# An FFN kernel with LoRA experts: two transposes per pair of token tiles moved from TensorE to VectorE and SBUF transfers

## The chip, the cores and the metric

The kernel runs on one core of a Trainium2 chip. The metric is the device time of one execution in microseconds (us). The kernel before takes 154.13 us, the median of 3 runs (153.89 to 154.21).

## The reference, cut to what matters

There are 2048 tokens of width 1024 (x, 32 x 64 x 1024, float32). Cut to its core, the reference is:

```
base   = x @ W.T                                   # 1024 x 1024
logits = x @ Wr.T + 5 * one_hot(id)                # 8 experts
gates  = softmax over the two largest logits, 0 elsewhere
h      = x @ A[e].T                                # 8 experts x rank 16 = 128 columns
cond   = base + 2 * sum_e gates[e] * (h[e] @ B[e].T)
out    = x + (cond @ V) @ (U * S).T                # rank 256
```

All is float32. The kernel keeps that precision by splitting each factor into a high part (float32r) and a low part, and by three products for each one: high by high, high by low, low by high.

## The kernel before, in words

Tokens are worked in 16 tiles of 128, two to a pair, so there are 8 pairs (0 to 7). First, for some 30 us, the kernel multiplies W by V into `proj` (1024 x 256), since cond @ V is x @ (W.T V) plus the LoRA part. `proj_hi` and `proj_lo` also hold A and Wr, so one product gives h (128 columns), logits (8) and the first half of z (128 columns, "z" is cond @ V of a token). From then on each pair goes through these stages, and TensorE's program (lines 525 to 561) is one fixed order of them:

- `project(t)` (line 388): for tile t, 8 chunks of 3 matmuls of 264 columns into the bank `pj0` or `pj1`: h, logits and z's first half, with tokens on the partitions.
- `half_t(p)` (line 405): z's second half for both tiles, 24 matmuls of 256 columns, made with z's features on the partitions, into the bank `zt`. Inside it, line 414 has two TensorE transposes that turn z's first half (copied by ScalarE to `z_sb`, line 637) into the same bank.
- `gates_top(t)` and `gates_apply(t)` on VectorE (lines 750 to 782): logits, the two largest, their softmax, and `gh`, which is h times its gates. The exponential is ScalarE's (line 641).
- `transpose_gh(p)` (line 422): two TensorE transposes of `gh` into the bank `gt`; ScalarE and VectorE split the result into `ghT_hi` (line 633) and `ghT_lo` (line 786).
- `mix(p)` (line 430): the LoRA part, 6 matmuls of 256 columns that add ghT times `bv` (B by V) to `zt`. It stands in `project(2p+2)` of the next pair, behind chunk 4.
- From `zt` ScalarE and VectorE make `zh` and `zl`, the high and low parts of seven combinations of the four 128 x 128 blocks (`split_za`, `sums`, `split_zb`, lines 607 to 623 and 793 to 817): the output product of a pair is done in Strassen's way, with 7 block products in place of 8.
- `first_part(p-2)` and `second_part(p-2)` (lines 493 to 502): in pair p's slot, 5 and then 2 of the block products of pair p-2, each 3 matmuls of 512 columns, into the four banks `fin`.
- `up`, `xb1`, `xa0`, `xb0`, `xa1` on VectorE (lines 819 to 847) and `sides` on GpSimd (line 306) add the products to `x_all`; SyncE stores it.

So TensorE's order in pair p is project(2p) with mix(p-1) inside, first_part(p-2), project(2p+1), second_part(p-2), half_t(p), transpose_gh(p). Each engine's order is written out by hand, and all waits are on semaphores. The splits of the transposed x (`xT_hi`, `xT_lo`) are ScalarE's line 591 and GpSimd's line 281, one tile of 128 x 1024 at a time. SyncE issues all loads and stores of the main loop (lines 242 to 250), in one order, with waits in between.

Of the kernel before, what the change touches and what calls it, by code (L numbers as in the profile page):

```python
# [16 lines left out]
def adaln_ffn(nc, xt, x, ids, VW, W, AW, B, U, S, out):  # L17
# [28 lines left out]
    with ExitStack() as ctx:  # L46
# [49 lines left out]
        zs = sb("zs", [P, 5, P], F32)  # L96
# [3 lines left out]
        b_raw = w_flat[:, 0:OC * ER].rearrange("p (c n) -> p c n", c=OC)  # L100
        u_raw = w_flat[:, OC * ER:OC * ER + MC * O].rearrange("p (m o) -> p m o", m=MC)
# [11 lines left out]
        gt_both = gt[:, 0:2 * P]  # L113
        bv_ps = gt[:, RANK:2 * RANK]
        zt_v = zt[:, :].rearrange("p (m t n) -> p m t n", m=MC, t=2)
# [41 lines left out]
        gt_done = sem("gt_done")  # L157
        gt_hi = sem("gt_hi")
# [3 lines left out]
        x22_copied = sem("x22_copied")  # L162
# [18 lines left out]
        LAG = 4  # L181
        PRODS = 7
# [12 lines left out]
        def _(sp):  # L195
# [74 lines left out]
        def _(pool):  # L270
# [20 lines left out]

            def make_tsum(j):
# [48 lines left out]
        def _(pe):  # L341
# [46 lines left out]
            def project(t):  # L388
                q, r = t % 2, t % XTR
                pe.wait_ge(xt_lo, t + 1)  # L390
                if t >= 2:
                    pe.wait_ge(gh_done, t - 1)
                    pe.wait_ge(z_copied, t - 1)
                for k in range(DC):
# [6 lines left out]
                    if t >= 2 and t % 2 == 0 and k == MH:  # L401
                        mix(t // 2 - 1)
                last.then_inc(pj_done, 1)

            def half_t(p):
                r = (2 * p) % XTR
                dst = zt_v[:, 1, :, :]
                for k in range(DC):
                    last = triple(dst, proj_hi[:, k, TCOLS:COLS], proj_lo[:, k, TCOLS:COLS],
                                  xT_hi[:, r:r + 2, k, :], xT_lo[:, r:r + 2, k, :], k == 0, False, shared=True)  # L410
                    if k == MH + 1:
                        pe.wait_ge(z_copied, 2 * p + 2)
                        for t in range(2):
                            nc.tensor.matmul(zt_v[:, 0, t, :], z_sb[:, t, :], ident[:, :], start=False, stop=False,  # L414
                                             is_transpose=True, skip_group_check=True)
                last.then_inc(xt_used, 1)

            def zt_free(p):
                pe.wait_ge(za_lo, p)
                pe.wait_ge(sums_done, 4 * p)  # L420

            def transpose_gh(p):
                pe.wait_ge(gh_done, 2 * p + 2)
                if p >= 1:
                    pe.wait_ge(gt_lo, p)
                for t in range(2):
                    last = nc.tensor.transpose(gt[:, t * P:(t + 1) * P], gh[:, t, :], ident[:, :])  # L427
                last.then_inc(gt_done, 1)

            def mix(p):  # L430
# [24 lines left out]
            def p1(p):  # L455
                pe.wait_ge(za_lo, p + 1)
                if p == 0:
                    pe.wait_ge(us_lo_done, 1)
                free_bank(p, 4)
                product(p, bank_a, 0, *us(0, 0), True, False)  # L460

            def p6(p):
                pe.wait_ge(zb_lo, p + 1)
                if p == 0:
                    pe.wait_ge(tl_done, 1)
# [65 lines left out]
            for p in range(1, PAIRS):  # L531
# [19 lines left out]
            pe.wait_ge(za_lo, PAIRS)  # L551
# [13 lines left out]
        def _(act):  # L565
# [41 lines left out]
            def split_za(p):  # L607
                act.wait_ge(zt_done, p + 1)
                zh_free(p)
                nc.scalar.copy(zh[:, p % 2, 0:MC, :], zt_v[:, :, 0, :]).then_inc(za_hi, 1)  # L610

            def split_zb_plain(p):
                act.wait_ge(za_lo, p + 1)
                nc.scalar.copy(zh[:, p % 2, MC:2 * MC, :], zt_v[:, :, 1, :]).then_inc(zb_hi, 1)

            def copy_x22(p):
                if p >= 1:
                    act.wait_ge(zb_lo, p)
                nc.scalar.copy(zs[:, 0, :], zt_v[:, 1, 1, :]).then_inc(x22_copied, 1)

            def split_zb(p):
                act.wait_ge(sums_done, 4 * p + 4)
                nc.scalar.copy(zh[:, p % 2, 2:7, :], zs[:, :, :]).then_inc(zb_hi, 1)
# [19 lines left out]
            def pair(p):  # L643
                if p < PAIRS - 1:
                    split_x(2 * p + 2)
                split_za(p - 1)
                copy_x22(p - 1)
                copy_u(p - 2)
                copy_z(2 * p)
                exp_top(2 * p)  # L650
                split_zb(p - 1)
                if p < PAIRS - 1:
                    split_x(2 * p + 3)
                copy_z(2 * p + 1)
                exp_top(2 * p + 1)
                split_gh(p)
# [43 lines left out]
            copy_x22(0)  # L700
            split_t(1)
            copy_z(2)
            exp_top(2)
            split_zb(0)
            copy_z(3)
            exp_top(3)
            split_x(5)
            split_gh(1)
# [8 lines left out]
        def _(dve):  # L717
# [48 lines left out]

            def gates_apply(s):
# [16 lines left out]
            def split_gh(p):  # L784
                dve.wait_ge(gt_hi, p + 1)
                nc.vector.tensor_sub(ghT_lo[:, :], gt_both, ghT_hi[:, :].bitcast(F32)).then_inc(gt_lo, 1)
# [6 lines left out]
            def split_za(p):  # L793
                dve.wait_ge(za_hi, p + 1)
                if p < PAIRS - 1:
                    dve.wait_ge(x22_copied, p + 1)
                nc.vector.tensor_sub(zl[:, p % 2, 0:MC, :], zt_v[:, :, 0, :],
                                     zh[:, p % 2, 0:MC, :].bitcast(F32)).then_inc(za_lo, 1)

            def split_zb_plain(p):  # L800
                dve.wait_ge(zb_hi, p + 1)
                nc.vector.tensor_sub(zl[:, p % 2, MC:2 * MC, :], zt_v[:, :, 1, :],
                                     zh[:, p % 2, MC:2 * MC, :].bitcast(F32)).then_inc(zb_lo, 1)

            def sums(p):
# [3 lines left out]
                nc.vector.tensor_sub(zs[:, 2, :], zs[:, 1, :], zt_v[:, 0, 0, :]).then_inc(sums_done, 1)  # L809
                dve.wait_ge(sums_done, n + 2)  # L810
                nc.vector.tensor_sub(zs[:, 3, :], zs[:, 0, :], zs[:, 2, :]).then_inc(sums_done, 1)
                nc.vector.tensor_sub(zs[:, 4, :], zt_v[:, 1, 0, :], zs[:, 2, :]).then_inc(sums_done, 1)

            def split_zb(p):
                dve.wait_ge(zb_hi, p + 1)
                nc.vector.tensor_sub(zl[:, p % 2, 2:7, :], zs[:, :, :],
                                     zh[:, p % 2, 2:7, :].bitcast(F32)).then_inc(zb_lo, 1)
# [35 lines left out]

            def pair_2():
                split_zb(0)
                split_us(1)
                split_za(1)
                up(0, 1)
                up(0, 2)
                xb1(0)  # L860
                sums(1)
                gates_top(4)
                gates_apply(4)
                gates_top(5)
                gates_apply(5)
# [3 lines left out]
                split_gh(2)  # L869
# [48 lines left out]
            sums(0)  # L918
            gates_top(2)
            gates_apply(2)  # L920
            gates_top(3)
            gates_apply(3)
            split_t(1)
            split_gh(1)
            pair_2()
            for p in range(3, PAIRS):
                pair(p)
            p = PAIRS - 2
# [52 lines left out]
```

## Time and profile before

| what | value |
|---|---|
| median of 3 runs | 154.13 us |
| the profiled execution | 153.88 us, its span 152.1 us |
| TensorE matmul busy | 147.3 us (97%), 1056 matmuls |
| VectorE busy | 107.3 us (71%) |
| GpSimd busy | 72.4 us (48%) |
| ScalarE busy | 63.6 us (42%) |
| DMA | 32.72 MB, mean 215 GB/s |
| granted TensorE clock | full in every slice |

The span is the stretch that the profiler records, and the execution's own time has 1.8 us around it. A matmul's duration in a row includes its pipeline, so back-to-back matmuls overlap: what one costs is the distance from its start to the next one's. VectorE's and ScalarE's rows overlap their neighbours by a little under 0.1 us in the same way.

### The profile page before, as it was taken

Reading aid. Unit: us, or ns where it says so; the run is one execution under the profiler, and the core shown is the slowest. Engines: PE = TensorE matmul, PEld = TensorE weight load, DVE = VectorE, ACT = ScalarE, POOL = GpSimd, SP = SyncE. Lnnn points to the kernel's source line nnn. Section 1 sums busy time; section 2 is a strip of 40 time slices with the busy share of each in tenths; the row PEclk is TensorE's granted clock in tenths of the full one; section 3 lists DMA queues with packets and bytes.
Section 4 is the critical chain, followed back from the end, with each engine's and each line's share of the span. In section 5 each row is a group of like instructions: output and inputs, shape, how many; then the busy total and the mean of one; then the engine's idle time right before and its main releaser. Section 6 shows DMA issues by size and latency. Waiting matters only on the chain.

```text
span 152.1 us, 2911 instructions
## 1 busy us (share of the span) xinstructions
PE 147.3 (97%) x1056; PEld 139.0 (91%) x1056; DVE 107.3 (71%) x297; ACT 63.6 (42%) x141; POOL 72.4 (48%) x57
## 2 busy tenths in 40 slices
PE   7899999999999999999999999999999999999991
PEld 5699999999999989998999899999999998998880
DVE  0787895769578999978755875596558736795851
ACT  4768867884637423346113612351334105013000
POOL 2000433992660659292966276646655640721800
PEclk9999999999999999999999999999999999999999
DMA  5999999999203040059629903980582067006184
GB/s 170 370 401 409 399 410 409 408 406 410 93 4 138 0 138 4 0 222 350 255 87 351 380 15 154 343 332 5 222 234 100 0 278 260 20 0 276 69 340 142
DMA packets 10669, 32.72 MB, mean 215 GB/s; under 512 B 1440, under 2 KB 1952, under 8 KB 10528
## 3 DMA queue, kind: packets, MB, share of 16 engines
q1 hardware_dynamic: 10368, 31.96, 56.0%
q10 hardware_dynamic: 288, 0.59, 1.0%
q8 instruction: 8, 0.13, 0.3%
q14 instruction: 5, 0.04, 0.1%
HBM read 24.16 MB, written 8.39 MB: 214 GB/s over the span
## 4 chain that ended last, share of the span: by engine, by line
PE 93%; DMA 3%; DVE 1%; ACT 0%; SPq 0%; issue 0%; DVEq 0%
PE fin L343 14%; PE fin L345 13%; PE fin L344 13%; PE pj L344 10%; PE pj L343 10%; PE pj L345 10%; PE zt L343 6%; PE zt L345 6%; PE zt L344 6%; DMA w_raw<-in_W 3%; PE gt L427 1%; PE zt L414 1%; PE gt L344 1%; PE gt L345 1%; PE gt L343 1%; DVE w_lo L722 0%
## 5 line engine op out<-in xcount | busy, mean ns | idle before, releaser
L281 POOL TENSOR_TENSOR xT_lo<-xt_raw,xT_hi 128x1024 fp32r<-128x1024 f32 x15 | 36.6, 2441 | 25.2 <-DVE gh L779 7.9
L304 POOL TENSOR_TENSOR x_all<-x_all,vw_raw 128x512 f32<-128x512 f32 x21 | 26.6, 1298 | 25.8 <-DVE vw_raw L827 25.8
L343 PE MATMUL pj<-proj_hi,xT_hi 128*128 128x264 f32 x128 | 36.9, 288 | 0.0
L344 PE MATMUL pj<-proj_lo,xT_hi 128*128 128x264 f32 x128 | 36.3, 284 | 0.0
L345 PE MATMUL pj<-proj_hi,xT_lo 128*128 128x264 f32 x128 | 36.2, 283 | 0.0
L343 PE MATMUL fin<-v_hi,w_hi 128*128 128x256 f32 (+1 forms) x88 | 28.0, 319 | 0.4 <-DVE w_lo L722 0.4
L344 PE MATMUL fin<-v_lo,w_hi 128*128 128x256 f32 (+1 forms) x88 | 27.9, 317 | 0.0
L345 PE MATMUL fin<-v_hi,w_lo 128*128 128x256 f32 (+1 forms) x88 | 27.9, 317 | 0.0
L344 PEld LDWEIGHTS pj<-proj_lo,xT_hi 128*128 128x128 f32 x128 | 24.1, 189 | 0.2
L343 PEld LDWEIGHTS pj<-proj_hi,xT_hi 128*128 128x128 f32 x128 | 24.1, 188 | 0.2
L345 PEld LDWEIGHTS pj<-proj_hi,xT_lo 128*128 128x128 f32 x128 | 24.0, 188 | 0.0
L343 PE MATMUL zt<-xT_hi,proj_hi 128*128 128x256 f32 x64 | 18.6, 291 | 0.0
L343 PEld LDWEIGHTS fin<-v_hi,w_hi 128*128 128x128 f32 x88 | 16.8, 190 | 1.5 <-DVE w_lo L722 0.6
L344 PE MATMUL zt<-xT_lo,proj_hi 128*128 128x256 f32 x64 | 17.9, 280 | 0.0
L345 PE MATMUL zt<-xT_hi,proj_lo 128*128 128x256 f32 x64 | 17.9, 280 | 0.0
L833 DVE TENSOR_TENSOR x_all<-fin,x_all 128x512 f32<-128x512 f32 x28 | 17.9, 682 | 0.0
L345 PEld LDWEIGHTS fin<-v_hi,w_lo 128*128 128x128 f32 x88 | 16.8, 191 | 1.2
L344 PEld LDWEIGHTS fin<-v_lo,w_hi 128*128 128x128 f32 x88 | 16.8, 191 | 0.8
L591 ACT CAST xT_hi<-xt_raw 128x1024 fp32r<-128x1024 f32 x16 | 16.8, 1049 | 0.6 <-DMA xt_raw<-in_xt 0.6
L637 ACT COPY z_sb<-pj 128x128 f32<-128x128 f32 x16 | 4.3, 266 | 22.4 <-DVE logit L754 22.4
L344 PEld LDWEIGHTS zt<-xT_lo,proj_hi 128*128 128x128 f32 x64 | 12.0, 188 | 0.3
L343 PEld LDWEIGHTS zt<-xT_hi,proj_hi 128*128 128x128 f32 x64 | 12.0, 188 | 0.2
(94 smaller groups left out, 275.1 us busy)
## 6 DMA issues: line engine op xcount, KB each, us to landing
xt_raw<-in_xt SPq DMA_DIRECT2D x16, 512.0 KB, 6.9
x_all<-in_x SPq DMA_DIRECT2D x16, 512.0 KB, 6.2
out<-x_all SPq DMA_DIRECT2D x13, 512.0 KB, 2.9
vw_raw<-in_VW SPq DMA_DIRECT2D x6, 384.0 KB, 7.4
w_raw<-in_W SPq DMA_DIRECT2D x8, 256.0 KB, 6.5
out<-x_all SPq DMA_DIRECT2D x5, 256.0 KB, 2.0
w_raw<-in_U SPq DMA_DIRECT2D x1, 1024.0 KB, 8.7
aw_raw<-in_AW SPq DMA_DIRECT2D x1, 544.0 KB, 7.6
```

The costliest lines, as they stand in the source:

```text
L281: nc.gpsimd.tensor_sub(xT_lo[:, t % XTR, :, :], xt_raw[:, t % XTR, :, :], xT_hi[:, t % XTR, :, :].bitcast(F32)).then_inc(xt_lo, 1)
L304: nc.gpsimd.tensor_add(x_all[:, t % XR, cols], x_all[:, t % XR, cols], ups[:, j, :]).then_inc(side_add, 1)
L343: nc.tensor.matmul(dst, l_hi, r_hi, start=first, stop=False, skip_group_check=shared)
L344: nc.tensor.matmul(dst, l_hi, r_lo, start=False, stop=False, skip_group_check=shared)
L345: return nc.tensor.matmul(dst, l_lo, r_hi, start=False, stop=last, skip_group_check=shared)
L414: nc.tensor.matmul(zt_v[:, 0, t, :], z_sb[:, t, :], ident[:, :], start=False, stop=False, is_transpose=True, skip_group_check=True)
L427: last = nc.tensor.transpose(gt[:, t * P:(t + 1) * P], gh[:, t, :], ident[:, :])
L591: nc.scalar.copy(xT_hi[:, t % XTR, :, :], xt_raw[:, t % XTR, :, :]).then_inc(xt_hi, 1)
L637: nc.scalar.copy(z_sb[:, t % 2, :], pj[t % 2][:, Z0:TCOLS]).then_inc(z_copied, 1)
L833: nc.vector.tensor_add(x_all[:, t % XR, cols], src[:, :], x_all[:, t % XR, cols]).then_inc(fin_read, 1)
```

## The change

z's first half and `gh` of pairs 1 to 5 are no longer transposed by TensorE. VectorE transposes them in 32 x 32 blocks within their place (`turn_z`, `turn_gh`) into `blk`; twelve SBUF-to-SBUF transfers on SyncE's queue (`move_blocks`) carry the blocks off the diagonal to their places in `tr`, and ScalarE copies the four on the diagonal (`move_diagonal`). `split_gh_moved` then splits gh's part of `tr`, and z's part is added to `zt` in `sums`. Pairs 0, 6 and 7 keep TensorE's transposes. `zt` becomes two banks used in turn, the second being `gt`. The LoRA part `mix(p-1)` of pairs 1 to 5 now stands behind `second_part(p-2)`, and pair 6's in `project(15)`. All seven combinations are split in one instruction of 896 columns instead of 256 and 640. GpSimd splits x in halves of 512 columns, two of them behind new waits, on `sums_done` and on `zb_lo`.

```diff
 # SyncE, main loop, p from 1
+            def move_blocks(p):
+                sp.wait_ge(blk_done, 3 * p)
+                for i in range(SQS):
+                    for j in range(SQS):
+                        if i != j:
+                            sp.dma_start(tr[SQ * j:SQ * (j + 1), p % 2, :, SQ * i:SQ * (i + 1)],
+                                         blk[SQ * i:SQ * (i + 1), p % 2, :, SQ * j:SQ * (j + 1)]).then_inc(tr_load, 16)
...
+                if p < TURNED:
+                    move_blocks(p)
                 if p >= 2:
                     store_pair(p - 2)
 # GpSimd
             for p in range(2, PAIRS):
+                if p >= 3:
+                    pool.wait_ge(zb_lo, p - 1)
+                    split_x_half(2 * p + 1, 1)
                 if p < PAIRS - 1:
-                    split_x(2 * p + 2)
+                    split_x_halves(2 * p + 2)
                 sides(p - 2)
                 if p < PAIRS - 1:
-                    pool.wait_ge(gh_done, 2 * p + 2)
-                    split_x(2 * p + 3)
+                    pool.wait_ge(sums_done, 4 * p)
+                    split_x_half(2 * p + 3, 0)
 # TensorE
                 if p >= 2:
                     second_part(p - 2)
+                if 2 <= p <= TURNED:
+                    mix(p - 1)
                 zt_free(p)
                 half_t(p)
-                transpose_gh(p)
+                if p >= TURNED:
+                    transpose_gh(p)
...
             def p1(p):
-                pe.wait_ge(za_lo, p + 1)
                 if p == 0:
+                    pe.wait_ge(za_lo, 1)
                     pe.wait_ge(us_lo_done, 1)
+                else:
+                    pe.wait_ge(zb_lo, p + 1)
 # ScalarE
+            def copy_half(p):
+                act.wait_ge(zt_done, p + 1)
+                act.wait_ge(zb_lo, p)
+                nc.scalar.copy(zs[:, 1:3, :], zt_v[p % 2][:, 1, :, :]).then_inc(z_half_copied, 1)
...
+            def split_gh_moved(p):
+                act.wait_ge(tr_load, MOVES * p)
+                act.wait_ge(tr_diag, SQS * p)
+                nc.scalar.copy(ghT_hi[:, :], tr[:, p % 2, 0:2, :]).then_inc(gt_hi, 1)
+            def move_diagonal(p):
+                act.wait_ge(blk_done, 3 * p)
+                for i in range(SQS):
+                    rows = slice(SQ * i, SQ * (i + 1))
+                    nc.scalar.copy(tr[rows, p % 2, :, rows], blk[rows, p % 2, :, rows]).then_inc(tr_diag, 1)
...
             def pair(p):
                 if p < PAIRS - 1:
                     split_x(2 * p + 2)
-                split_za(p - 1)
-                copy_x22(p - 1)
                 copy_u(p - 2)
-                copy_z(2 * p)
+                if p >= TURNED:
+                    copy_z(2 * p)
                 exp_top(2 * p)
-                split_zb(p - 1)
                 if p < PAIRS - 1:
                     split_x(2 * p + 3)
-                copy_z(2 * p + 1)
-                exp_top(2 * p + 1)
-                split_gh(p)
+                    split_gh_moved(p - 1)
+                    if p == TURNED:
+                        copy_z(2 * p + 1)
+                    exp_top(2 * p + 1)
+                    copy_half(p - 1)
+                    split_zb(p - 1)
+                    if p < TURNED:
+                        move_diagonal(p)
+                    else:
+                        split_gh(p)
 # VectorE
+            def turn_z(t):
+                nc.vector.transpose(blk[:, (t // 2) % 2, 2 + t % 2, :], pj[t % 2][:, Z0:TCOLS]).then_inc(blk_done, 1)
+            def turn_gh(p):
+                dve.wait_ge(gh_done, 2 * p + 2)
+                nc.vector.transpose(blk[:, p % 2, 0:2, :], gh[:, :, :]).then_inc(blk_done, 1)
+            def split_gh_moved(p):
+                dve.wait_ge(gt_hi, p + 1)
+                nc.vector.tensor_sub(ghT_lo[:, :].rearrange("p (t n) -> p t n", t=2), tr[:, p % 2, 0:2, :],
+                                     ghT_hi[:, :].bitcast(F32).rearrange("p (t n) -> p t n", t=2)).then_inc(gt_lo, 1)
             def sums(p):
                 n = 4 * p
-                nc.vector.tensor_add(zs[:, 1, :], zt_v[:, 0, 1, :], zs[:, 0, :]).then_inc(sums_done, 1)
+                dve.wait_ge(zt_done, p + 1)
...
+                dve.wait_ge(z_half_copied, p)
+                if p < TURNED:
+                    nc.vector.tensor_add(zs[:, 0:8:7, :], zt_v[p % 2][:, 0, :, :], tr[:, p % 2, 2:4, :]).then_inc(z0_done, 1)
+                else:
+                    nc.vector.tensor_copy(zs[:, 0:8:7, :], zt_v[p % 2][:, 0, :, :]).then_inc(z0_done, 1)
+                dve.wait_ge(z0_done, p)
+                nc.vector.tensor_add(zs[:, 3, :], zs[:, 7, :], zs[:, 2, :]).then_inc(sums_done, 1)
...
+            def gates(t):
+                gates_top(t)
+                if 2 <= t < 2 * TURNED:
+                    turn_z(t)
+                gates_apply(t)
+
+            def gates_and_gh(t):
+                gates_top(t)
+                if t < 2 * TURNED:
+                    turn_z(t)
+                split_gh_moved(t // 2 - 1)
+                gates_apply(t)
             def pair_2():
                 split_zb(0)
                 split_us(1)
-                split_za(1)
                 up(0, 1)
                 up(0, 2)
                 xb1(0)
+                gates(4)
+                gates_and_gh(5)
+                turn_gh(2)
                 sums(1)
...
             def pair(p):
-                split_zb(p - 2)
-                split_za(p - 1)
-                sums(p - 1)
-                gates_top(2 * p)
-                gates_apply(2 * p)
+                gates(2 * p)
                 up(p - 2, 1)
                 up(p - 2, 2)
                 xb1(p - 2)
                 xa0(p - 2)
-                gates_top(2 * p + 1)
-                gates_apply(2 * p + 1)
+                gates_and_gh(2 * p + 1)
+                if p < TURNED:
+                    turn_gh(p)
+                sums(p - 1)
                 xb0(p - 2)
                 xa1(p - 2)
-                if p == PAIRS - 1:
-                    split_zb(p - 1)
-                split_gh(p)
+                split_zb(p - 1)
```

TURNED is 6. The order of the last pair, and the first one's `sums_first`, which works from PSUM as before, are cut from the diff above.

## Rows read from the trace of the kernel before

**Rows 1.** Chain that ended last: share of the span by engine.
```profile
PE 93%; DMA 3%; DVE 1%; ACT 0%; SPq 0%; issue 0%; DVEq 0%
```
**Rows 2.** Waits of TensorE: who for whom, us in total, times, longest.
```profile
PE fin L343 <- DVE w_lo L722: 0.4, 1, 0.4
```
**Rows 3.** Chain in order of time, one pair's transposes: start, us on the chain.
```profile
78.22 0.22 PE zt L414 x2
79.15 0.22 PE gt L427 x2
```
**Rows 4.** Timeline of TensorE, pairs 3 and 4: start, us, line, out<-in, count.
```profile
74.55 0.40 PE L343 MATMUL fin<-v_hi,w_hi 128*128 128x512 f32 x1
75.93 0.28 PE L343 MATMUL zt<-xT_hi,proj_hi 128*128 128x256 f32 x1
...
78.99 0.39 PE L427 MATMUL gt<-ident,gh 128*128 128x128 f32 x2
...
81.01 0.28 PE L343 MATMUL zt<-ghT_hi,bv_hi 128*128 128x256 f32 x1
...
81.72 0.28 PE L343 MATMUL pj<-proj_hi,xT_hi 128*128 128x264 f32 x1
...
82.81 0.40 PE L343 MATMUL fin<-us_hi,w_hi 128*128 128x512 f32 x1
...
85.54 0.39 PE L343 MATMUL fin<-us_hi,w_hi 128*128 128x512 f32 x1
```
**Rows 5.** Timeline of VectorE, pairs 3 and 4.
```profile
74.75 0.16 DVE L754 SCALAR_TENSOR_TENSOR logit<-target,pj 128x8 f32<-128x8 f32 x1 [0.80 <-PE pj L345]
...
79.81 0.42 DVE L786 TENSOR_TENSOR ghT_lo<-gt,ghT_hi 128x256 fp32r<-128x256 f32 x1 [1.60 <-ACT ghT_hi L633]
80.16 0.82 DVE L816 TENSOR_TENSOR w_lo<-zs,w_hi 128x640 fp32r<-128x640 f32 x1
...
82.90 0.28 DVE L807 TENSOR_TENSOR zs<-zt,zs 128x128 f32<-128x128 f32 x1
...
83.95 0.15 DVE L754 SCALAR_TENSOR_TENSOR logit<-target,pj 128x8 f32<-128x8 f32 x1
...
84.46 0.23 DVE L759 TENSOR_SCALAR dtop<-top 128x2 f32<-128x2 f32 x1
...
84.87 0.18 DVE L762 TENSOR_TENSOR chosen<-iota_e,top_i 128x16 f32<-128x16 f32 x1
...
85.53 0.35 DVE L779 SCALAR_TENSOR_TENSOR gh<-pj,rsum,gate 128x128 f32<-128x128 f32 x1
85.80 1.51 DVE L827 TENSOR_TENSOR vw_raw<-fin,vw_raw 128x512 f32<-128x512 f32 x2
```
**Rows 6.** Timeline of GpSimd, pairs 2 and 4.
```profile
57.21 3.83 POOL L304 TENSOR_TENSOR x_all<-x_all,vw_raw 128x512 f32<-128x512 f32 x3
...
86.56 3.79 POOL L304 TENSOR_TENSOR x_all<-x_all,vw_raw 128x512 f32<-128x512 f32 x3 [3.33 <-DVE vw_raw L827]
```
**Rows 7.** Timeline of VectorE in pair 2, beside the first row of group 6.
```profile
59.27 0.55 DVE L759 TENSOR_SCALAR dtop<-top 128x2 f32<-128x2 f32 x1
...
59.99 1.09 DVE L762 TENSOR_TENSOR chosen<-iota_e,top_i 128x16 f32<-128x16 f32 x1
```
**Rows 8.** Timeline of ScalarE.
```profile
70.39 0.71 ACT L623 CAST w_hi<-zs 128x640 fp32r<-128x640 f32 x1
...
79.41 0.37 ACT L633 CAST ghT_hi<-gt 128x256 fp32r<-128x256 f32 x1 [3.25 <-PE gt L427]
```
**Rows 9.** Timeline of TensorE, its one wait on VectorE.
```profile
6.61 0.39 PE L343 MATMUL fin<-v_hi,w_hi 128*128 128x256 f32 x1 [0.43 <-DVE w_lo L722]
6.83 0.28 PE L344 MATMUL fin<-v_lo,w_hi 128*128 128x256 f32 x1
```
**Rows 10.** SyncE's queue: issues, start and us.
```profile
12.08 1.01 SPq L233 DMA_DIRECT2D s_col<-in_S  x1
...
65.93 0.43 SPq L213 DMA_DIRECT2D out<-x_all  x1
```
**Rows 11.** DMA queue 1 (packets, MB, share of 16 engines); then issues (KB, us to landing).
```profile
q1 hardware_dynamic: 10368, 31.96, 56.0%
...
out<-x_all SPq DMA_DIRECT2D x2, 128.0 KB, 1.9
```

More of the change, by code:

```diff
@@ L112, in adaln_ffn @@
         zt = bank("zt")
[L113 removed]
         bv_ps = gt[:, RANK:2 * RANK]
[L115 removed]
+        zt_bank = [zt, gt]
+        zt_v = [b[:, :].rearrange("p (m t n) -> p m t n", m=MC, t=2) for b in zt_bank]
         vw_load = [sem(f"vw_load{k}") for k in range(OC)]
@@ L181, in adaln_ffn @@
         LAG = 4
+        TURNED = PAIRS - 2
+        SQ = 32
+        SQS = P // SQ
+        MOVES = 16 * SQS * (SQS - 1)
         PRODS = 7
@@ L400, in project @@
                                   proj_hi[:, k, 0:TCOLS], proj_lo[:, k, 0:TCOLS], k == 0, k == DC - 1)
-                    if t >= 2 and t % 2 == 0 and k == MH:
-                        mix(t // 2 - 1)
+                    if t == 2 and k == MH:
+                        mix(0)
+                    if t == LAST and k == MH:
+                        mix(TURNED)
                 last.then_inc(pj_done, 1)
@@ L410, in half_t @@
                                   xT_hi[:, r:r + 2, k, :], xT_lo[:, r:r + 2, k, :], k == 0, False, shared=True)
-                    if k == MH + 1:
-                        pe.wait_ge(z_copied, 2 * p + 2)
+                    if k == MH + 1 and (p == 0 or p >= TURNED):
+                        pe.wait_ge(z_copied, 2 if p == 0 else 2 * (p - TURNED) + 4)
                         for t in range(2):
-                            nc.tensor.matmul(zt_v[:, 0, t, :], z_sb[:, t, :], ident[:, :], start=False, stop=False,
+                            nc.tensor.matmul(zt_v[p % 2][:, 0, t, :], z_sb[:, t, :], ident[:, :], start=False, stop=False,
                                              is_transpose=True, skip_group_check=True)
@@ L418, in zt_free @@
             def zt_free(p):
-                pe.wait_ge(za_lo, p)
-                pe.wait_ge(sums_done, 4 * p)
+                if p == 1:
+                    pe.wait_ge(bv_lo_done, 1)
+                if p == 2:
+                    pe.wait_ge(za_lo, 1)
+                if p >= 2:
+                    pe.wait_ge(sums_done, 4 * (p - 1))
+                if p >= 3:
+                    pe.wait_ge(z_half_copied, p - 2)
             def transpose_gh(p):
+                dst = gt if p in (0, TURNED) else pj[0]
                 pe.wait_ge(gh_done, 2 * p + 2)
-                if p >= 1:
-                    pe.wait_ge(gt_lo, p)
+                if p == TURNED:
+                    pe.wait_ge(sums_done, 4 * p)
+                    pe.wait_ge(z_half_copied, p - 1)
                 for t in range(2):
-                    last = nc.tensor.transpose(gt[:, t * P:(t + 1) * P], gh[:, t, :], ident[:, :])
+                    last = nc.tensor.transpose(dst[:, t * P:(t + 1) * P], gh[:, t, :], ident[:, :])
                 last.then_inc(gt_done, 1)
@@ L462, in p6 @@
             def p6(p):
-                pe.wait_ge(zb_lo, p + 1)
                 if p == 0:
+                    pe.wait_ge(zb_lo, 1)
                     pe.wait_ge(tl_done, 1)
@@ L631, in split_gh @@
             def split_gh(p):
-                act.wait_ge(gt_done, p + 1)
-                nc.scalar.copy(ghT_hi[:, :], gt_both).then_inc(gt_hi, 1)
+                act.wait_ge(gt_done, 1 if p == 0 else p - TURNED + 2)
+                nc.scalar.copy(ghT_hi[:, :], (gt if p in (0, TURNED) else pj[0])[:, 0:2 * P]).then_inc(gt_hi, 1)
             def copy_z(t):
@@ L645, in pair @@
                     split_x(2 * p + 2)
-                split_za(p - 1)
-                copy_x22(p - 1)
                 copy_u(p - 2)
-                copy_z(2 * p)
+                if p >= TURNED:
+                    copy_z(2 * p)
                 exp_top(2 * p)
-                split_zb(p - 1)
                 if p < PAIRS - 1:
                     split_x(2 * p + 3)
-                copy_z(2 * p + 1)
-                exp_top(2 * p + 1)
-                split_gh(p)
+                    split_gh_moved(p - 1)
+                    if p == TURNED:
+                        copy_z(2 * p + 1)
[6 more added lines that the diff above has]
+                        split_gh(p)
+                else:
+                    copy_half(p - 1)
+                    split_zb(p - 1)
+                    copy_z(2 * p + 1)
+                    exp_top(2 * p + 1)
+                    split_gh(p)
             first = RANK + P
@@ L785, in split_gh @@
                 dve.wait_ge(gt_hi, p + 1)
-                nc.vector.tensor_sub(ghT_lo[:, :], gt_both, ghT_hi[:, :].bitcast(F32)).then_inc(gt_lo, 1)
+                nc.vector.tensor_sub(ghT_lo[:, :], (gt if p in (0, TURNED) else pj[0])[:, 0:2 * P],
+                                     ghT_hi[:, :].bitcast(F32)).then_inc(gt_lo, 1)
+            def split_gh_moved(p):
+                dve.wait_ge(gt_hi, p + 1)
+                nc.vector.tensor_sub(ghT_lo[:, :].rearrange("p (t n) -> p t n", t=2), tr[:, p % 2, 0:2, :],
+                                     ghT_hi[:, :].bitcast(F32).rearrange("p (t n) -> p t n", t=2)).then_inc(gt_lo, 1)
             def split_t(b):
@@ L812, in sums @@
-                nc.vector.tensor_sub(zs[:, 4, :], zt_v[:, 1, 0, :], zs[:, 2, :]).then_inc(sums_done, 1)
+                nc.vector.tensor_sub(zs[:, 5, :], zs[:, 2, :], zs[:, 4, :]).then_inc(sums_done, 1)
+                nc.vector.tensor_sub(zs[:, 6, :], zs[:, 1, :], zs[:, 4, :]).then_inc(sums_done, 1)
             def split_zb(p):
                 dve.wait_ge(zb_hi, p + 1)
-                nc.vector.tensor_sub(zl[:, p % 2, 2:7, :], zs[:, :, :],
-                                     zh[:, p % 2, 2:7, :].bitcast(F32)).then_inc(zb_lo, 1)
+                first = 2 if p == 0 else 0
@@ L819, in up @@
+                nc.vector.tensor_sub(zl[:, p % 2, first:7, :], zs[:, first:7, :],
+                                     zh[:, p % 2, first:7, :].bitcast(F32)).then_inc(zb_lo, 1)
             def up(p, j):
@@ L880, in pair, with last_pair @@
                 xa0(p - 2)
-                gates_top(2 * p + 1)
-                gates_apply(2 * p + 1)
+                gates_and_gh(2 * p + 1)
+                if p < TURNED:
+                    turn_gh(p)
+                sums(p - 1)
                 xb0(p - 2)
                 xa1(p - 2)
-                if p == PAIRS - 1:
-                    split_zb(p - 1)
+                split_zb(p - 1)
+            def last_pair(p):
+                split_gh(p - 1)
+                gates(2 * p)
+                up(p - 2, 1)
+                up(p - 2, 2)
+                xb1(p - 2)
+                xa0(p - 2)
+                sums(p - 1)
+                gates(2 * p + 1)
+                split_zb(p - 1)
+                xb0(p - 2)
+                xa1(p - 2)
                 split_gh(p)
@@ L917, in _ @@
             split_za(0)
[L918 to L922, printed above, removed]
+            sums_first()
+            gates(2)
+            gates(3)
+            turn_gh(1)
             split_t(1)
-            split_gh(1)
             pair_2()
-            for p in range(3, PAIRS):
+            for p in range(3, PAIRS - 1):
                 pair(p)
+            last_pair(PAIRS - 1)
             p = PAIRS - 2
```

74 lines of the change are left out of this document (45 added, 29 removed).

## The prediction

> **What bounds the kernel now.** I read the chain that ended last first: TensorE holds 93% of the span [rows 1]. Then its waits: the only one on another engine's split data is 0.4 us, near the start [rows 2, 9], so no stage of any pair makes TensorE wait. Whatever leaves TensorE is therefore worth its full time, and whatever makes TensorE wait costs its full time. Third the timelines of a pair. TensorE's stages, start to start [rows 4]: second_part 75.93 - 74.55 = 1.38 us; half_t with its transposes 78.99 - 75.93 = 3.06; mix 81.72 - 81.01 = 0.71; nine matmuls of a project 82.81 - 81.72 = 1.09, so 24 of them 2.9; four block products 85.54 - 82.81 = 2.73, so five 3.42. The kernel's other engines all run beside it.
>
> **What is removed.** Two transposes of z and two of gh stand on the chain with 0.22 us a couple [rows 3], the same in every pair. Pairs 1 to 5 lose both: 5 x 0.44 = 2.2 us. A changed pair without waits is 2 x 2.9 + 3.42 + 1.38 + 0.71 + 2.84 = 14.15 us against 14.58.
>
> At this place the Trainium skill speaks against the edit: "VectorE: DVE Perf Modes", Rules for kernel authors, says to let TensorE do a 128 x 128 transpose where PSUM as a target will do, and to use VectorE for 32 x 32 blocks. Its table gives 311 ns for a VectorE pass over 128 x 128 (bf16); by that a pair would get 4 x 0.31 = 1.2 us more on VectorE for 0.44 us less on TensorE. The rows say only what TensorE's part costs.
>
> **What is added: the wait of mix.** This is the step that decides. mix(p-1) now stands right behind second_part(p-2), 1.38 us after project(2p+1) ends. It waits for gt_lo, which is VectorE's split_gh_moved(p-1), and that stands behind gates_top(2p+1) and turn_z(2p+1), which can't start before project(2p+1) ends. Call F the start of second_part (74.55 in pair 3). VectorE's logit row starts at F + 0.20 [rows 4, 5]. From logit to the chosen row's end without hindrance: 84.87 + 0.18 - 83.95 = 1.10 [rows 5], so F + 1.30. turn_z: the trace has no VectorE transpose. Bounds: an 8-column row, 0.15, and a 512-column one from PSUM, 0.75 (1.51 for two) [rows 5]; nearest is the 128-column row 0.28 (line 807) [rows 5], which I take; its start overlaps its neighbour, so it ends at F + 1.50. The subtraction of 256 columns lasts 0.42 (line 786) [rows 5], so F + 1.85. TensorE then restarts: its one such wait has the second matmul 0.22 behind the first where 0.12 is usual [rows 9], so 0.10 for the pipeline and 0.05 for the signal. mix could go at F + 1.38 and goes in effect at F + 2.00: at least 0.62 us of wait in each of mixes 1 to 5, 3.1 us, which alone is more than the 2.2 us saved. Behind mix on TensorE's queue stand half_t and everything else; nothing covers it.
>
> **GpSimd in the way of VectorE.** The floor holds only if no VectorE instruction is held up. GpSimd's three side additions run from 57.21 to 61.04, 1.27 us each [rows 6]. VectorE's line 759, usually 0.23, lasts 0.55 and ends at 59.82, just when the second addition ends; line 762, usually 0.18, lasts 1.09 and ends at 61.08, just when the third ends [rows 5 to 7]. So a VectorE row with both inputs in SBUF, or line 759's kind, that meets a GpSimd one waits for that to finish; a row that reads PSUM doesn't (the two line-827 rows at 85.80 keep their length beside GpSimd's from 86.56). The Trainium skill agrees: "SBUF — State Buffer", Who interferes with whom, says that a VectorE instruction with two SBUF inputs and a GpSimd one that reads SBUF exclude each other for the whole instruction; its rule gives the same times as the rows.
>
> The change makes all sums, the gh split and an 896-column split such rows, and moves GpSimd's x halves. I follow one steady pair from e, the end of split_gh_moved(p-1), with a GpSimd half at 1.27 us:
> - gh of tile 2p+1 is done at e + 0.75, turn_gh (256 columns, 0.42; bounds 0.15 and 0.75 again) at e + 1.21. mix's last matmul ends at e + 1.05, copy_half (0.37) [rows 8] at e + 1.45, the new 256-column addition (0.42) at e + 1.91, the four sums (1.13, from 82.90 to the next line's start and 0.08 of overlap) [rows 5] at e + 3.07.
> - GpSimd's half (2p+3, 0) follows at e + 3.15 to 4.42; xb0 and xa1 hide it. The split of 896 columns: 0.82 for 640 and 0.27 more for 256, behind ScalarE's 0.71 + 0.22; held until 4.42, it ends at e + 5.38. p1 needs it at e + 6.6: no wait there, 1.2 us to spare.
> - Then GpSimd runs three halves in a row: e + 5.45 to 6.72, 7.99, 9.26. TensorE ends project(2p+2) at e + 0.15 + 0.71 + 2.84 + 2.9 = 6.6, VectorE's line 759 is due at e + 7.3 and waits until 7.99, line 762 until 9.26. gates_apply ends at 10.26, up starts at 10.18, and GpSimd's sides 0.76 later [rows 5, 6]: e + 10.94 to 12.21, 13.47, 14.73.
> - The next F is e + 12.9. Its line 759 is due at 13.6 and waits for the third side, 14.73; then line 762, turn_z and the split end at e' = e + 15.65.
>
> So the loop through VectorE and GpSimd, not TensorE, sets the period: 15.65 us against TensorE's 14.15, a wait of 1.5 us per mix. In this loop line 759 misses the gap between two sides by 0.14 us; where it gets in, 0.3 us less. I take half of that off four pairs, 0.6 us.
>
> **Pair 2** is its own case: VectorE does up, up, xb1 before gates(4), while GpSimd still has x halves until 57.0 and the sides until 60.8. F is 59.96 in the trace of before and 58.8 now (0.44 and one mix, 0.71, less before it). gates(4) ends at about 61.3, split_gh_moved(1) at 62.9; mix(1) was due at 60.2: 2.85 us (bounds 0.6, if nothing is held, and 4). The others: 1.7 (pair 3), 1.5, 1.5, and 1.1 for pair 6, which has no turn_z. The sum of waits is 2.85 + 1.7 + 1.5 + 1.5 + 1.1 = 8.65, less 0.6 = 8.05 us.
>
> **The transfers.** move_blocks(p) is issued at e + 1.3, twelve on SyncE's queue at 0.43 to 1.01 each [rows 10]: 5.2 to 12 us; nearest is 0.43, as the other DMAs of 128 pieces. Small transfers land 1.9 us after issue [rows 11]: e + 8.4. They are needed by ScalarE's split_gh_moved(p) at e + 14.8, so 6 us to spare. Each has 128 pieces of 128 bytes, 96 per DMA engine for the twelve. The trace has no such pieces; bounds are nothing and a usual piece, 0.56 x 16 x 152.1 / 10368 = 0.13 us, thus 12.6 us, landing at e + 15.8, a little late. store_pair and the loads queue behind the moves on SyncE; they come some 7 us later in the pair, but their data is wanted a pair later. ScalarE's four diagonal copies (some 0.25 each) stand before its x split, which has 1 us to spare to GpSimd's half.
>
> **The ends.** Pair 7: sums(6) now comes between project(15) and its gates; zb_lo is ready at about F + 4.35 where p1(6) is due at 4.65, and split_gh(7) at 5.9 where mix(7) is due at 6.0. I cost it at 0 (bounds 0 and 0.5).
>
> **Sum.** On the profiled execution, 153.88 us (span 152.1 and 1.8 around it): - 2.2 + 8.05 = + 5.85, 159.7 us. The median is 0.25 above that execution, so 160.0 us.
>
> **Rivals.**
> - *Only the direct wait* (0.62 x 5 = 3.1, no collision with GpSimd in the gates): 154.13 - 2.2 + 3.1 = 155.0 us, up to 156.5 with some collisions. For it: the GpSimd starts in the loop rest on ten estimates in a row. Against: lines 759 and 762 are met well inside the halves.
> - *Faster*: gt_lo is there before second_part ends, and every wait is hidden: 154.13 - 2.2 = 151.9 us. It decides from a wait of mix below 0.44 us on average. Against it: the 1.65 us that four VectorE steps need after a logit that comes 1.18 us before mix is due. For it: only that the rows of before don't show a VectorE transpose, nor this order.
> - *Late moves*: pieces slower than 0.13 us, or issues at 1 us and more, pass the 6 us to spare; each us beyond costs 4 to 5 us in all, so about 165 us for one.
> - *Slow VectorE transposes*, 0.56 for 128 columns: both turn_z and 0.14 of turn_gh lie in the loop, 0.7 us per pair, 163 us.
>
> **How the numbers follow.** The forecast has a chance of 0.57, with 158 to 161.5 as its own range; only the direct wait 0.22; faster 0.07; late moves 0.06; slow transposes 0.08. The range from 155.0 to 163.0 leaves out the faster case, late moves and little else. A measurement tells 0.2% (0.3 us) from no change: faster 0.07, same 0.03, slower 0.90.
>
> **What would show it.** Right: TensorE's waits have the first matmul of mix five times on VectorE's ghT_lo, 1 to 3 us each; lines 759 and 762 last up to 1.1 us and end with a GpSimd row; pair to pair is some 15.6 us from pair 3 to 5. The moves land 7 to 9 us after turn_gh. Wrong: waits of mix of about 0.6 us (the first rival), a project or p1 that waits instead, ScalarE's ghT_hi waiting for a DMA (late moves), or transposes on VectorE that last 0.5 us and more.

## The result and the profile after

The changed kernel takes 161.94 us, the median of 5 runs (161.59 to 162.26), against 154.16 us for the kernel before: 1.0502 times as long, 95% interval 1.048 to 1.0525. The profiled execution took 161.9 us, its span 160.1, which is 8.0 us more than the span before. Of all executions reported here one was slow (165.26 us, of the kernel without transfers); ranges and ratios leave it out.

Its chain that ended last, by engine, where before TensorE had 93% [rows 1]:

```profile
PE 77%; DVE 15%; DMA 3%; issue 2%; DVEq 1%; ACT 0%; SPq 0%
```

TensorE's waits on VectorE (us in total, times, longest), against the one line of [rows 2]:

```profile
PE gt L371 <- DVE ghT_lo L868: 5.3, 3, 3.1
PE zt L371 <- DVE ghT_lo L868: 2.7, 2, 1.4
PE fin L371 <- DVE w_lo L792: 1.4, 1, 1.4
```

Line 868 is `split_gh_moved`, and five waits on it are the five mixes behind second_part (the target alternates between the banks `gt` and `zt`). Here they are in TensorE's timeline; ahead of each stands the start of second_part's last product, three matmuls of 0.23 us and so 0.69 us before mix was due:

```profile
60.64 0.39 PE L371 MATMUL fin<-us_hi,w_hi 128*128 128x512 f32 x1
64.57 0.38 PE L371 MATMUL gt<-ghT_hi,bv_hi 128*128 128x256 f32 x1 [3.09 <-DVE ghT_lo L868]
...
78.15 0.39 PE L371 MATMUL fin<-us_hi,w_hi 128*128 128x512 f32 x1
80.39 0.39 PE L371 MATMUL zt<-ghT_hi,bv_hi 128*128 128x256 f32 x1 [1.40 <-DVE ghT_lo L868]
...
93.98 0.39 PE L371 MATMUL fin<-us_hi,w_hi 128*128 128x512 f32 x1
96.12 0.39 PE L371 MATMUL gt<-ghT_hi,bv_hi 128*128 128x256 f32 x1 [1.30 <-DVE ghT_lo L868]
...
109.66 0.39 PE L371 MATMUL fin<-us_hi,w_hi 128*128 128x512 f32 x1
111.84 0.39 PE L371 MATMUL zt<-ghT_hi,bv_hi 128*128 128x256 f32 x1 [1.34 <-DVE ghT_lo L868]
...
125.41 0.39 PE L371 MATMUL fin<-us_hi,w_hi 128*128 128x512 f32 x1
127.21 0.39 PE L371 MATMUL gt<-ghT_hi,bv_hi 128*128 128x256 f32 x1 [0.96 <-DVE ghT_lo L868]
```

A mix that started on time would stand 0.69 behind the row above it. So they are late by 3.24, 1.55, 1.45, 1.49 and 1.11 us, 8.84 in all. Each loses 0.10 more behind its first matmul: the second follows after 0.22 to 0.23 us where 0.12 is usual. That makes 9.35 us. (The idle times in brackets add up to less, 8.1 us, since they count from the modelled end of the matmul before.) With 2.2 us less for transposes that is + 7.15. Another 1.1 us is at the very start: this execution's first piece of W's second half landed that much later. The end, from the last matmul on, is 0.3 us shorter. That makes the 8.0.

Why ghT_lo is late is in VectorE's timeline of pair 4, beside GpSimd's:

```profile
87.70 0.79 DVE L829 TENSOR_SCALAR dtop<-top 128x2 f32<-128x2 f32 x1
...
88.66 1.09 DVE L832 TENSOR_TENSOR chosen<-iota_e,top_i 128x16 f32<-128x16 f32 x1
89.67 0.30 DVE L838 STREAM_TRANSPOSE w_raw<-pj 128x128 f32<-128x128 f32 x1
...
93.49 0.16 DVE L824 SCALAR_TENSOR_TENSOR logit<-target,pj 128x8 f32<-128x8 f32 x1 [0.19 <-PE pj L373]
93.75 0.17 DVE L827 MAX8 top<-logit 128x8 f32<-128x8 f32 x1
94.01 1.18 DVE L829 TENSOR_SCALAR dtop<-top 128x2 f32<-128x2 f32 x1
...
95.69 0.38 DVE L868 TENSOR_TENSOR ghT_lo<-w_raw,ghT_hi 128x256 fp32r<-128x256 f32 x1
```

```profile
85.93 3.80 POOL L308 TENSOR_TENSOR xT_lo<-xt_raw,xT_hi 128x512 fp32r<-128x512 f32 x3 [1.03 <-DVE w_lo L918]
91.36 3.80 POOL L329 TENSOR_TENSOR x_all<-x_all,vw_raw 128x512 f32<-128x512 f32 x3 [1.64 <-DVE vw_raw L929]
```

GpSimd's three x halves and its three side additions last some 1.27 us each. The even tile's line 829 ends with GpSimd's second half, at 88.5, its line 832 with the third, at 89.7. That sends `up` (line 929), and with it GpSimd's side additions, back so far that the odd tile's line 829, on two elements, lasts 1.18 us and ends with the third addition, at 95.16. The split, line 868, stands behind these rows. The next even tile's logit row stands at 102.86, 15.68 us after this pair's at 87.18.

### The profile page after: what moved, and what is told of

The parts are those of the page before. It is cut to its first block, busy times and chain, and to the rows that moved or that the text cites. A ratio compares the mean times of both kernels' runs of the same rounds, so it can differ in the third digit from the quotient of the medians.

```text
span 160.1 us, 2968 instructions
## 1 busy us (share of the span) xinstructions
PE 146.6 (92%) x1036; PEld 136.5 (85%) x1036; DVE 121.2 (76%) x312; ACT 67.9 (42%) x145; POOL 73.5 (46%) x67
## 4 chain that ended last, share of the span: by engine, by line
PE 77%; DVE 15%; DMA 3%; issue 2%; DVEq 1%; ACT 0%; SPq 0%
PE fin L371 10%; PE fin L373 10%; PE fin L372 10%; PE pj L372 9%; PE pj L371 8%; PE pj L373 8%; PE gt L371 4%; DVE dtop L829 4%; PE gt L373 4%; PE gt L372 4%; PE zt L371 3%; DMA w_raw<-in_W 3%; PE zt L372 3%; PE zt L373 3%; DVE chosen L832 2%
## 5 line engine op out<-in xcount | busy, mean ns | idle before, releaser
L308 POOL TENSOR_TENSOR xT_lo<-xt_raw,xT_hi 128x512 fp32r<-128x512 f32 x22 | 28.5, 1314 | 43.3 <-DVE w_raw L913 21.3
L302 POOL TENSOR_TENSOR xT_lo<-xt_raw,xT_hi 128x1024 fp32r<-128x1024 f32 x5 | 12.3, 2475 | 13.5 <-ACT xT_hi L637 7.9
L702 ACT ACTIVATE etop<-dtop 128x2 f32<-128x2 f32 x16 | 3.3, 205 | 21.7 <-DVE dtop L829 21.5
L371 PE MATMUL fin<-us_hi,w_hi 128*128 128x512 f32 (+1 forms) x31 | 11.8, 379 | 0.0
L372 PE MATMUL fin<-us_lo,w_hi 128*128 128x512 f32 (+1 forms) x31 | 11.7, 376 | 0.0
L373 PE MATMUL fin<-us_hi,w_lo 128*128 128x512 f32 (+1 forms) x31 | 11.6, 376 | 0.0
L829 DVE TENSOR_SCALAR dtop<-top 128x2 f32<-128x2 f32 x16 | 10.4, 649 | 1.5
```

The costliest lines, as they stand in the source:

```text
L302: nc.gpsimd.tensor_sub(xT_lo[:, t % XTR, :, :], xt_raw[:, t % XTR, :, :], xT_hi[:, t % XTR, :, :].bitcast(F32)).then_inc(xt_lo, 1)
L308: op = nc.gpsimd.tensor_sub(xT_lo[:, t % XTR, ks, :], xt_raw[:, t % XTR, ks, :], xT_hi[:, t % XTR, ks, :].bitcast(F32))
L371: nc.tensor.matmul(dst, l_hi, r_hi, start=first, stop=False, skip_group_check=shared)
L372: nc.tensor.matmul(dst, l_hi, r_lo, start=False, stop=False, skip_group_check=shared)
L373: return nc.tensor.matmul(dst, l_lo, r_hi, start=False, stop=last, skip_group_check=shared)
L702: nc.scalar.activation(etop[:, :], dtop[:, :], ACT.Exp, accum_out=esum[:, :]).then_inc(exp_done, 1)
```

## The experiments

All ratios are to the kernel before, run on the same chip.

**The split moved ahead of the gates.** `e1_early`:

```diff
 # VectorE, pair(p); the same in pair_2
+                split_gh_moved(p - 1)
                 gates_and_gh(2 * p + 1)
 # in gates_and_gh
-                split_gh_moved(t // 2 - 1)
```

> The changed kernel with one step moved: VectorE's split_gh_moved(p-1) before gates_top(2p+1), no longer behind it. Theory A (the loop of VectorE and GpSimd sets the period): mix finds its input in time from pair 3 on, but the collisions stay, the loop only gets shorter by the 0.3 us of the split, and TensorE waits somewhere else, at p1 or a project; period about 15.2 us, the whole about 160 us. Theory B (only the order of the split and gates_top costs): the waits of mix, 9.4 us in all in the changed kernel's profile, are gone save that of mix(1), about 3 us: 155.5 us or less.

Measured: 156.51 us (156.17 to 157.73), 1.0132 (1.0092 to 1.0172). The waits view has one wait on VectorE's split in the main loop, that of mix(1):

```profile
PE gt L371 <- DVE ghT_lo L868: 1.8, 1, 1.8
```

Pairs 3 to 6 follow at 14.15, 14.4 and 14.7 us, the start of second_part standing at 78.12, 92.27, 106.71 and 121.41. What makes the last two longer than 14.15 is a short wait at `p1`, the first product of first_part, and in the last also one at mix. At the first of these p1 waits for VectorE's 896-column split, which ends at 100.18:

```profile
98.97 1.21 DVE L918 TENSOR_TENSOR w_lo<-w_raw,w_hi 128x896 fp32r<-128x896 f32 x1
100.23 0.19 PEld L371 LDWEIGHTS fin<-us_hi,w_hi 128*128 128x128 f32 x1 [0.17 <-DVE w_lo L918]
```

So the step moved is worth 5.4 us, more than theory A gave it. A's loop through VectorE and GpSimd is there, and TensorE meets it at p1 as A said, but it is near 14.7 us and not 15.2. B's number is nearer, but B is not right either, as the next run shows. The line-868 rows now meet side additions themselves (0.96 us where 0.38 is usual). In pairs 3 and 4 they have time for it; in pairs 5 and 6 they end 0.05 us before mix starts, which is then 0.13 and 0.19 us late.

**GpSimd's rows made short.** `e3_pool_short`; in the main loop the outputs lack most of the side additions and of x's low parts (the diff is shortened):

```diff
-tensor_add(x_all[:, t % XR, cols], x_all[:, t % XR, cols], ups[:, j, :])
+tensor_add(x_all[:, t % XR, n * BANK:n * BANK + 8], ..., ups[:, j, 0:8])
-tensor_sub(xT_lo[:, t % XTR, ks, :], ...)
+tensor_sub(xT_lo[:, t % XTR, ks, 0:2], ...)
```

> The changed kernel with GpSimd's work in the main loop cut to 8 columns per side addition and 8 per x half; semaphores and order stay (the output lacks these parts). Theory A: no VectorE row waits for GpSimd, each mix still waits the 0.62 us of its order: 161.9 - 9.4 + 3.1 = 155.6 us. Theory B: GpSimd doesn't matter: 161.9 us.

Measured: 154.96 us (154.37 to 155.71), 1.0044 (1.0022 to 1.0067). Order and semaphores of the changed kernel are all there, and 7 of its 7.8 us are gone; the time is 0.6 below what was expected. TensorE's waits on line 868 (869 in this file):

```profile
PE gt L372 <- DVE ghT_lo L869: 1.1, 3, 0.4
PE zt L372 <- DVE ghT_lo L869: 0.7, 2, 0.4
```

These are five idle times of 0.36 us. What a wait costs TensorE is more, by the starts of its matmuls at pair 4's mix:

```profile
89.41 0.39 PE L374 MATMUL fin<-us_hi,w_lo 128*128 128x512 f32 x1
90.15 0.39 PE L372 MATMUL gt<-ghT_hi,bv_hi 128*128 128x256 f32 x1 [0.35 <-DVE ghT_lo L869]
90.38 0.28 PE L373 MATMUL gt<-ghT_lo,bv_hi 128*128 128x256 f32 x1
```

mix starts 0.74 behind the matmul before it, where 0.23 is usual, and its second matmul 0.23 behind the first, where 0.12 is usual: 0.51 + 0.10 = 0.61 us, five times, and 3.1 us in all (the last is 0.67). The distance from this mix to the one before, 14.78 us, is 14.15 + 0.61 within 0.02. That is the floor that the order sets, and the 0.62 of the forecast. In pair 4 VectorE's gate rows run unhindered from the logit to the split:

```profile
88.46 0.16 DVE L825 SCALAR_TENSOR_TENSOR logit<-target,pj 128x8 f32<-128x8 f32 x1 [1.37 <-PE pj L374]
88.72 0.17 DVE L828 MAX8 top<-logit 128x8 f32<-128x8 f32 x1
88.98 0.23 DVE L830 TENSOR_SCALAR dtop<-top 128x2 f32<-128x2 f32 x1
...
89.71 0.38 DVE L869 TENSOR_TENSOR ghT_lo<-w_raw,ghT_hi 128x256 fp32r<-128x256 f32 x1
```

**Which of GpSimd's rows.** `e2_sides_short` has only the side additions short (the outputs lack them) and the x halves in full:

> The changed kernel with GpSimd's side additions cut to 8 columns (the output lacks them) and its x halves in full. Theory A, split by place: the rows of the odd tile's gates no longer meet a side addition, the even tile's still meet the x halves, which only delays up and not mix: 0.5 us of wait in mixes 2 to 5, some 1.5 us in mix(1), whose gates(4) still meets x halves: 155.5 us. If the x halves are what costs: above 159 us.

Measured: 154.70 us (154.67 to 154.74, three runs), 1.0039 (1.0023 to 1.0055), 0.8 below the number expected, with waits on line 868 of 1.1 and 0.9 us in five. The side additions are what makes mix wait longer than its order does. The x halves still hold the even tile's line 829 up (0.84 us at 97.73), which only pushes `up` back, and nothing waits for that here. mix(1) started 0.51 us late, as with all of GpSimd's rows short, and not 1.5.

**Both edits.** `e4_pool_short_early`, e1 and e3 together (same parts left out):

> Both edits: GpSimd's work short (left out of the output as before) and split_gh_moved before gates_top. Both theories: mix waits for nothing, TensorE alone sets the pace, what is left of the change is the 2.2 us less on TensorE: 151.9 us, or 153.0 us if the 1.1 us by which the first matmul on W's second half was late in the profile of the changed kernel belongs to the change.

Measured: 152.09 us (151.6 to 152.63), 0.9865 (0.9822 to 0.9908). The waits view has no wait on VectorE left. With both costs gone the change gains 2.1 us; 2.2 was counted from the chain for the ten couples of transposes. The profile's shorter end (0.3) and a p1 held for 0.2 in pair 3 are in it too and nearly cancel.

**No transfers.** `e5_no_moves`; the outputs lack the blocks off the diagonal of pairs 1 to 5:

```diff
-                if p < TURNED:
-                    move_blocks(p)
 # split_gh_moved on ScalarE
-                act.wait_ge(tr_load, MOVES * p)
+                act.wait_ge(blk_done, 3 * p)
 # sums
-                    dve.wait_ge(tr_load, MOVES * p)
```

> The changed kernel without the 60 SBUF transfers and the waits on them; the blocks off the diagonal are not moved (the output lacks them). Theory A: the transfers are hidden, they landed some 3.6 us before VectorE's split in pair 4; 161.9 us, within 0.5. Rival (transfers or SyncE's queue cost time): 160.5 us or less. If the late first transfer of W came from the transfers' presence in the program, another 1.1 us less.

Measured: 162.28 us (161.9 to 162.28), 1.0501 (1.045 to 1.0552), as the changed kernel. The transfers are hidden. They are not as cheap as forecast, though. Pair 3's batch in the changed kernel's SyncE queue, and its landing seen by ScalarE:

```profile
81.58 8.66 SPq L258 DMA_DIRECT2D w_raw<-w_raw  x12
...
91.70 0.41 ACT L678 CAST ghT_hi<-w_raw 128x256 fp32r<-128x256 f32 x1 [1.95 <-DMA w_raw<-w_raw]
```

That is 0.72 us per issue (0.64 and 0.66 in the batches after and before it) where 0.43 was taken. The batch lands 10.1 us after turn_gh ends (9.0 to 10.1 in the five pairs, where 7 to 9 was forecast). ghT_hi is ready at 92.11, 3.6 us before VectorE's split starts at 95.69. With the split moved ahead of the gates less is left: in pair 4 of `e1_early` ghT_hi is ready 0.17 us before the split starts.

**Gate rows that can't meet GpSimd.** `e7_psum_early` computes all of the reference, with GpSimd's full work. Besides e1's edit:

```diff
 # VectorE, gates_top and gates_apply, tiles 2 to 11; c = TCOLS, b = pj[t % 2]
-  max(top[:, :], logit)                      # top in SBUF
+  max(b[:, c + 24:c + 32], logit)            # top in PSUM, read by dtop and max_index
-  chosen[:, :, :] = (iota_e == top_i)
+  b[:, c + 8:c + 24] = (b[:, c:c + 8] == top_i)      # a copy of iota_e in PSUM
-  pick = chosen * etop                       # 128x16
-  gate = pick[:, 0] + pick[:, 1]
+  pick[:, 1] = chosen[:, 1] * etop[:, 1]     # tensor_scalar, chosen in PSUM
+  gate = chosen[:, 0] * etop[:, 0] + pick[:, 1]      # scalar_tensor_tensor
```

> The changed kernel with split_gh_moved before gates_top, and for tiles 2 to 11 the gate rows rewritten so that none has both inputs in SBUF or reads and writes SBUF alone: the two largest (top), a copy of the expert numbers (iota) and chosen lie in spare columns of the bank pj, pick is made for the second expert alone, and one scalar_tensor_tensor makes the gate. GpSimd does its full work. The output is complete. Theory A (mix's wait is 0.5 us of order, and the rest is gate rows waiting for GpSimd): no wait of mix is left, as with the short GpSimd rows; 152.0 to 152.8 us, faster than the kernel before. Theory C (GpSimd's rows slow VectorE whatever its rows read): as with the split moved alone, 156.5 us.

Measured: 152.60 us (152.54 to 152.62), 0.9902 (0.9885 to 0.9918): faster than both kernels, and 3.9 us below e1, from which only the gate rows differ. The even tile's rows of pair 4, under GpSimd's three halves from 80.98 to 84.77:

```profile
82.76 0.22 DVE L840 TENSOR_SCALAR dtop<-pj 128x2 f32<-128x2 f32 x1
...
83.17 0.18 DVE L844 TENSOR_TENSOR pj<-pj,top_i 128x16 f32<-128x16 f32 x1
```

```profile
80.98 3.79 POOL L316 TENSOR_TENSOR xT_lo<-xt_raw,xT_hi 128x512 fp32r<-128x512 f32 x3 [1.03 <-DVE w_lo L937]
```

0.22 and 0.18 us, their usual lengths, beside the same GpSimd work that stretched them to 0.79 and 1.09. Tile 12 in the same execution has the old rows, and there they are stretched as before, the second until GpSimd's halves end at 113.09:

```profile
111.05 0.80 DVE L840 TENSOR_SCALAR dtop<-top 128x2 f32<-128x2 f32 x1
...
112.03 1.09 DVE L844 TENSOR_TENSOR chosen<-iota_e,top_i 128x16 f32<-128x16 f32 x1
```

So GpSimd does not slow VectorE as such; what the VectorE row reads and writes decides. The edit moves inputs and outputs together, so which of the two counts in each row is not shown. One wait on the split is left, mix(1)'s of 0.44 us.

**The same gate rows, the split left where it was.** `e6_psum`:

> The same rewritten gate rows, split_gh_moved left behind gates_top and turn_z. Theory A: each of the five mixes waits the 0.5 us of its order, as with the short GpSimd rows: 154.6 to 155.2 us. Theory C: 161.9 us, as the changed kernel.

Measured: 155.92 us (155.47 to 156.46), 1.0113 (1.008 to 1.0146), some 0.7 above the range of theory A and far from C. The waits on the split are 2.5 us in five; four are the order's 0.35 to 0.45, and one of 1.0, in pair 6, is outside the tiles whose rows were changed. From start to start the five cost TensorE 3.8 us; less 2.2 for the transposes that is 1.6, and 1.8 was measured. A's range took 0.5 us per mix where the order costs 0.61, and had no longer wait in pair 6.

**The changed kernel again.** `e8_again`, unaltered:

> The changed kernel once more, unaltered. In its first profile the first project began 1.1 us later than in the kernel before's, and the clock stayed at full through the 3.1 us wait of mix(1); without the transfers the start was as before and the clock fell after a like wait. If the late start belongs to the change, project(0) begins at 29.4 us again; if it is chance from execution to execution, it may be anywhere from 28.2 to 29.8 us. The clock after mix(1)'s wait: full in both or fallen in this one, which says whether the fall is chance too. The time: 161.9 us, within 0.5.

Measured: 161.78 us (160.87 to 163.16), 1.0501 (1.0433 to 1.057). Its five waits are those of the first profile:

```profile
PE gt L371 <- DVE ghT_lo L868: 5.4, 3, 3.1
PE zt L371 <- DVE ghT_lo L868: 2.7, 2, 1.4
```

project(0) began at 28.46 us, against 29.42 in the first profile of the same program and 28.30 before. In the profiles of the other kernels it began between 28.19 and 29.81, with no relation to what was changed. So the late start varies from execution to execution, and the span's 1.1 us from it does not belong to the change.

## Why the prediction was right

The forecast was 160.0 us, slower, with 158 to 161.5 as the forecast's own range; 161.9 is inside the stated range of 155.0 to 163.0 and 0.4 above its inner one. The mechanism that it named is the one found; two sizes were off (the deduction for line 759 and mix(1)'s wait, both below), and part of the distance is not the change's. Of the 2.2 us between the forecast for the profiled execution, 159.7, and its 161.9, 1.3 are waits of mix, 1.1 the late start and - 0.3 the shorter end (0.1 is left over). By its steps:

- **Transposes, 2.2 us off TensorE.** Right: 2.1 by e4.
- **mix waits for VectorE's split, at least 0.62 us each.** Mechanism and size are right, in five places: 0.61 in e3, where GpSimd's rows are out of the way. There the split ends 1.83 us after second_part starts (88.26 to 90.09), and 1.85 was worked out.
- **GpSimd in VectorE's way.** Right. The loop of pairs 4 and 5 has 15.68 us where 15.65 was worked out; the side additions end 1.9 us after second_part starts (95.16, and 93.29), where 1.83 was worked out. e3 takes 7.0 us away by short GpSimd rows, e2 shows that the side additions are the part that counts, e7 that rows reading PSUM pass. By "SBUF — State Buffer" (Who interferes with whom) of the Trainium skill the second SBUF input and the two-port mode are what collide. e7 is a test of that rule, and its trace agrees: line 829's row and line 832's keep 0.22 and 0.18 us, where they last 0.79 and 1.09 in the changed kernel.
- **The waits' sum.** This term was mis-sized: 8.05 was forecast, 9.35 measured. 0.6 of the 1.3 is the deduction for line 759 (829 now) slipping between two side additions. It slips in pair 3, but then line 832 lasts 1.04 us and nothing is saved, and in the other pairs it doesn't slip. 0.5 is mix(1), 3.34 for 2.85: GpSimd's side additions in pair 2 start 0.7 us later than taken (at 58.82, which is 57.7 without the late start, for 57.0), behind an x split that lasts 2.74 us where 2.41 is usual. Four of tile 4's gate rows meet GpSimd there, one after another, and last 1.05 to 1.17 us each. The last 0.2 are the other four waits, 6.0 for 5.8.
- **VectorE's transposes, the one operation that no row of before showed.** 0.31 us for 128 columns and 0.45 for 256 where 0.28 and 0.42 were taken.
- **Transfers hidden.** Right by e5, with 3.6 us to spare and not 6, as an issue is 0.64 us and more. The sign named for late moves, ghT_hi waiting for a DMA, did appear, in four of the five pairs (0.5 to 1.9 us), and did no harm; it was not a good sign.
- **Pair 7 costs nothing.** Right: no wait there. The end is even 0.3 us shorter, which was not forecast and is not explained.

Of the rivals, "only the direct wait", 155.0 us, is what e3 measures, 154.96: the case would have come about with GpSimd out of the way. "Faster" came about, at 152.1 us (e4) and 152.6 (e7), only with both the order and the collisions taken away. The late moves and slow transposes did not occur.

What the forecast left out is the clock. In the first profile TensorE ran at full clock throughout, and so did the fastest execution of e8 (160.87 us, mean 1.000). Three more of e8's executions (161.74 to 163.16) had a mean of 0.989. The profile without transfers shows where that is, in windows of 2 us around mix(1)'s wait (busy time of each engine, then PEclk, DMA share, GB/s):

```profile
60.00:62.00 2.00, 0.38 (x2) 0.00 (x0) 1.93 (x4) 0.00 (x0) 1.65 (x2) 1.00 0.00 0
62.00:64.00 2.00, 0.35 (x1) 0.35 (x2) 1.71 (x13) 0.30 (x2) 0.00 (x0) 0.78 0.00 0
64.00:66.00 2.00, 2.00 (x11) 2.00 (x11) 0.93 (x3) 0.37 (x1) 0.00 (x0) 0.50 0.03 8
66.00:68.00 2.00, 2.00 (x17) 2.00 (x17) 1.90 (x7) 0.53 (x1) 0.48 (x1) 0.86 0.00 0
```

TensorE did nothing from 60.38 to 63.65. The granted clock fell to the lower level, 1.2 GHz, at about 63.1, within that time, and stayed there for some 3 us; the 30 matmuls of mix and half_t took 4.9 us where 3.7 is usual. That is 1.3 us. Four of the five executions in the result have a mean clock of 0.979 to 0.989, as this one has, so most timed executions of the changed kernel seem to have paid about as much; their traces are not there to show it. The 160.87 us of e8 had neither this nor the late start. In e1's profile the clock fell as well, at about 64.0, 0.3 us into a mix that had waited 1.84 us; in both profiles of the changed kernel it stayed full through a wait of 3.1. What decides is open.

## What to carry to other kernels

Where one engine is on the chain of waits all the time, ask of each step that is moved what it now stands behind on its own engine, and when the last of that can be ready; a saving of 2.2 us was lost to five waits, 9.35 us together, on a subtraction whose inputs had been ready for 3.5 to 4.6 us. On VectorE count a small row with two SBUF inputs beside a GpSimd row at the GpSimd row's length, 1.05 to 1.17 us here for 8 or 16 elements, and move such rows' operands to PSUM or GpSimd's rows away before the chain depends on them. Price a wait by the starts of the matmuls around it: an idle time of 0.35 us cost 0.61. The change is worth having once that is done: 152.6 us against 154.1.

## What the runs showed of the hardware

- A VectorE transpose of 32 x 32 blocks runs at the pace of other rows: 0.31 us for 128x128 from PSUM, 0.45 for 128x256, float32.
- An SBUF-to-SBUF transfer of 128 pieces of 128 bytes lands 1.8 us after issue (median of 60), counted from the issue's start. Twelve in a row cost SyncE 7.7 to 8.7 us of issue. Without all 60 the kernel was no faster (162.28 us for 161.94).
- VectorE's two-element row from SBUF to SBUF (dtop) lasts up to 1.26 us beside GpSimd's rows in the changed kernel, where 0.23 is usual. The same row reading PSUM takes 0.22 us in all ten tiles.
